# One GpSimd product per unit instead of two, softplus spread over three units, and gates behind the fourth scan, in a selective-scan kernel on one core

## What is computed

```python
x = x + 0.5 * ffn(layernorm(x))       # int4-quantized weight, bias, low-rank part
x = x + ssm(layernorm(x))             # below; 512 channels, 64 states each
x = x + 0.5 * ffn(layernorm(x))

# ssm, for each sequence
h = layernorm(x) * norm_w + norm_b
u, z = split(h @ Win)                 # 512 and 512 channels
u = silu(causal_conv4(u) + conv_b)
dt = softplus(u @ dt_w + dt_b)
B, C = u @ Bp, u @ Cp                 # 64 states each
state[d, s] = state[d, s] * exp(dt[d] * A[d, s]) + dt[d] * u[d] * B[s]    # over time
y[d] = sum_s state[d, s] * C[s]
out = x + ((y + u * D) * silu(z)) @ Wout
```

## Time and profile before

| | us |
|---|---|
| median of 3 runs | 5270.37 (5265.89 to 6636.7) |
| the profiled execution, its time | 5275.21 |
| its span, first to last instruction | 5272.6 |

### The profile page before, as it was taken

How to read it: one execution, slowest core, us unless ns; L and a number is a source line. 1 busy time by engine, 2 the same in 40 slices (tenths; PEclk the granted TensorE clock), 3 DMA queues, 4 the chain that set the end, 5 groups by cost and what they waited for, 6 DMA issues and landing times.

```text
span 5272.6 us, 189257 instructions
## 1 busy us (share of the span) xinstructions
PE 4814.2 (91%) x85070; PEld 2906.2 (55%) x85070; DVE 4915.5 (93%) x4674; ACT 3854.6 (73%) x6536; POOL 5021.0 (95%) x2312
## 2 busy tenths in 40 slices
PE   7989989899898999989999898998989989999887
PEld 4555555555555555555555555555555555555554
DVE  7999999999999999999999999999999999999996
ACT  5687777778777787777767778777787777766564
POOL 4999999999999999999999999999999999999997
PEclk8999999999999999999999999999999999999999
DMA  8755666556565565655656566565655656557543
GB/s 217 194 187 192 170 204 177 193 178 185 187 177 191 180 185 191 173 201 183 176 193 169 201 177 186 189 179 190 180 191 187 175 194 176 187 180 183 191 178 117
DMA packets 578058, 970.78 MB, mean 184 GB/s; under 512 B 294593, under 2 KB 328162, under 8 KB 511714
## 3 DMA queue, kind: packets, MB, share of 16 engines
q1 hardware_dynamic: 327394, 948.32, 56.4%
q10 hardware_dynamic: 249856, 10.36, 3.6%
HBM read 872.60 MB, written 85.98 MB: 182 GB/s over the span
## 4 chain that ended last, share of the span: by engine, by line
PE 35%; POOL 28%; DVE 20%; issue 10%; ACT 4%; DMA 3%; SPq 1%; DVEq 0%; POOLq 0%; ACTq 0%
POOL H L866 24%; DVE H L645 17%; PE pUB L972 14%; PE Y L998 12%; PE pP L936 3%; PE pP L930 3%; DVE cv L596 2%; ACT dA L422 2%; DMA Bd<-scratch_diag 2%; POOL dto L847 1%; POOL duo L853 1%; POOL lnv L842 1%; PE pA L1012 1%; DMA scratch_ut<-uto 1%; ACT L422 1%
## 5 line engine op out<-in xcount | busy, mean ns | idle before, releaser
L866 POOL TENSOR_TENSOR H<-H,Cb 128x1024 f32<-128x1024 f32 x2048 | 4782.6, 2379 | 151.1 <-DVE H L645 134.0
L645 DVE TENSOR_TENSOR_SCAN H<-dA,pUB 128x512 f32<-128x512 f32 x4096 | 4639.7, 1198 | 238.8 <-PE pUB L972 213.8
L422 ACT ACTIVATE dA<-DT,w_negA 128x512 f32<-128x512 f32 x4096 | 2620.1, 711 | 1230.9 <-DVE H L645 1227.2
L972 PEld LDWEIGHTS pUB<-Bd,UT 64*64 64x64 f32 x65536 | 1873.1, 134 | 1428.4 <-DVE H L645 682.7
L972 PE MATMUL pUB<-Bd,UT 64*64 64x128 f32 x65536 | 2243.4, 275 | 404.7 <-DVE H L645 321.5
L998 PE MATMUL Y<-H,w_ident 64*64 64x512 f32 x16384 | 1970.3, 595 | 9.9 <-POOL H L866 5.0
L998 PEld LDWEIGHTS Y<-H,w_ident 64*64 64x64 f32 x16384 | 599.5, 135 | 614.7 <-issue 601.7
L930 PE MATMUL pP<-hT,w_Win 128*128 128x512 f32 x480 | 239.3, 621 | 0.0
L936 PE MATMUL pP<-U,w_dt_w 128*128 128x512 f32 x480 | 238.1, 618 | 0.0
L422 ACT ACT_TABLE_LOAD x178 | 228.4, 1283 | 11.3 <-DVE H L645 4.7
L1012 PE MATMUL pA<-w_Wf,XNT 128*128 128x256 f32 x496 | 142.7, 412 | 7.5 <-DVE X L600 6.1
(11 more groups left out here) (151 smaller groups left out, 1750.3 us busy)
## 6 DMA issues: line engine op xcount, KB each, us to landing
Cb<-scratch_c SPq DMA_DIRECT2D x512, 1024.0 KB, 5.2
Bd<-scratch_diag SPq DMA_DIRECT2D x510, 512.0 KB, 6.2
ZL<-scratch_z SPq DMA_DIRECT2D x64, 256.0 KB, 6.7
scratch_z<-zo SPq DMA_DIRECT2D x62, 256.0 KB, 5.7
scratch_dt<-dto SPq DMA_DIRECT2D x60, 256.0 KB, 6.8
scratch_ut<-uto SPq DMA_DIRECT2D x60, 256.0 KB, 5.6
DT<-scratch_dt SPq DMA_DIRECT2D x60, 256.0 KB, 5.0
UT<-scratch_ut SPq DMA_DIRECT2D x60, 256.0 KB, 5.6
```

The lines of the kernel that those rows point to most:

```text
L422: last = nc.scalar.activation(dA[:, n % DAR, j, :], DT[:, k, :], ACT.Exp, scale=c["negA"][:, k, GS * blk + j:GS * blk + j + 1])
L645: last = nc.vector.tensor_tensor_scan(H[:, u % HR, 2 * i + j, :], dA[:, n % DAR, 2 * i + j, :], pUB[:, i, :].rearrange("p (t s) -> p s t", ...
L866: nc.gpsimd.tensor_tensor(h[:, j:j + 2, :], h[:, j:j + 2, :], Cb[:, blk % 2, j:j + 2, :], ALU.mult).then_inc(times_c, 1)
L972: last = nc.tensor.matmul(out, UT[rows, k, j * P + h * HP:j * P + h * HP + HP], Bd[rows, blk % 2, i, j * P:(j + 1) * P].rearrange("p (t s) ...
```

## The change

GpSimd waits for all four scans of a unit and multiplies the four states in one operation of 128x2048; `times_c` still rises by two per unit. The three softplus operations stand behind the products of three units (table POOLS: "less" at 32, 38, 46, 54, "dt" one unit later, "du" two later). The gates move from behind the second scan to behind the fourth, in the same units.

```diff
@@ -36,7 +36,7 @@
         "norm 3": (49, 50, 51, 55), "turn 1": (25, 27), "turn c": (38, 41), "turn 3": (58, 62)}
 DVES = {"norm 1": (6,), "norm c": (26,), "norm 2": (43,), "norm 3": (51,), "soft": (31, 37, 45, 53),
         "conv": (2, 7, 12, 17), "x2": (13, 20), "x1": (30, 34), "out": (44, 46)}
-POOLS = {"dt": (32, 38, 46, 54), "du": (33, 39, 47, 55)}
+POOLS = {"less": (32, 38, 46, 54), "dt": (33, 39, 47, 55), "du": (34, 40, 48, 56)}
 PES = {"xs": (0, 5, 10, 15), "z": (3, 8, 13, 18), "BC": ((20, 22),), "turn b": (24,), "dt": ((26, 28), (32, 34), (40, 42), (48, 50)),
        "turn u": (38, 46, 54, 59), "turn 1": (23, 25), "turn c": (36, 39), "turn 3": (56, 60)}
 LATER = {"y": ((7, 12), (17, 19)), "ffn 1": ((27, 29), (31, 33)), "ffn c": ((41, 43), (44, 45))}
@@ -603,10 +603,10 @@
 
                 c_, q, a = b - 1, b + 1, b + 2
                 when = DVES
-                if close and n == 3 and i == 1:
+                if close and n == 3 and i == 3:
                     gate(c_, 2)
                     gate(c_, 3)
-                if scan and n == HALF + 3 and i == 1:
+                if scan and n == HALF + 3 and i == 3:
                     gate(b, 0)
                     gate(b, 1)
                 if proj and n in when["conv"] and i:
@@ -860,14 +860,13 @@
                     if scan:
                         if n % 2 == 0:
                             pool.wait_ge(c_in[blk % 2], at(16 * (b * NBLK + n // 4 + 1)))
-                    for j in range(0, GS, 2):
-                        if scan:
-                            pool.wait_ge(state_done, at(2 * (GN * b + n) + j // 2 + 1))
-                            nc.gpsimd.tensor_tensor(h[:, j:j + 2, :], h[:, j:j + 2, :], Cb[:, blk % 2, j:j + 2, :], ALU.mult).then_inc(times_c, 1)
-                        if proj and n in when["dt"]:
-                            sum_dt(q, when["dt"].index(n), j // 2)
-                        if proj and n in when["du"] and j == 0:
-                            times_u(q, when["du"].index(n))
+                        pool.wait_ge(state_done, at(2 * (GN * b + n) + 2))
+                        nc.gpsimd.tensor_tensor(h, h, Cb[:, blk % 2], ALU.mult).then_inc(times_c, 2)
+                    for part, what in enumerate(("less", "dt")):
+                        if proj and n in when[what]:
+                            sum_dt(q, when[what].index(n), part)
+                    if proj and n in when["du"]:
+                        times_u(q, when["du"].index(n))
                     if close and n in turns["norm c"]:
                         shift_of(nc, pool, flipc, normc[0], normc[3], normc[4], c_)
                     if ffn and n in turns["norm 1"]:
```

## The result

The changed kernel takes 5186.56 us (median of four runs, 5184.62 to 5194.16) against 5270.61 us before: a ratio of 0.9846, with a 95% interval of 0.9829 to 0.9863. The ratio is that of the mean times, without one execution before that took 6636.7 us; the medians give 0.9841. That is 84 us less, where the sum said 78, and 5187 where 5192 was forecast. The profiled execution took 5194.16 us, its span 5192.2 against 5272.6.

A forecast was written before the change was run, and what follows sets the result against it. Each step was bound by VectorE and TensorE for units 0 to 37, then GpSimd for 38 to 61. 15 x (3.8 + 1.2) plus 3 gave 78 us less: 5192 us, range 5152 to 5262.

The forecast's parts named there:

- Price of the product: GpSimd's product with C: one 128x2048 operation takes 4.51 us against 4.648 for two, saving 0.14 us per unit.
- The rival in which nothing of the start is saved: GpSimd's product stays at 4.65 us per unit; the kernel takes 5260 us; chance 0.12.
- the one in which the long product is dearer: Units 32 to 61: product costs more than two short ones, kernel slower from 4.68 us, up to 5408; chance 0.07.
- Later entry: GpSimd waits for all four states of unit 32, so its stretch starts 2.1 us later each step.
- Phase two: GpSimd's stretch with softplus work, counted from unit 32 to 61: no waits, 1.3 us margin at unit 38, 3.8 us gained per step.
- Gate of unit 3: VectorE's wait for TensorE's last sum goes, 1.0 us a step, plus 0.2 for what follows.
- Softplus spread, SP's wait, the dt of ACT: Softplus over three units, SP's 1.2 us at unit 56's dt store, ACT's dt ready 0.8 us early: all cost nothing.
- The sums of odd units: TensorE's sums in odd units wait 2.3 us more for a whole product; covered, 1 us per step if not.
- The last step: Step without softplus, GpSimd's throughout: 9 us could go, VectorE's end caps it, less 2 us: 3 us gained.
- The signs: Expected in the trace: starts 4.51 us apart, more GpSimd idle before gapless units 32 to 61, gates' idle 15, chain entry near 32.
- Given back at the handover: Rival: transfers and SP's new wait hold units 60, 62, 66; half of 3.8 us lost, 5220 us; chance 0.16.
- more than summed: Rival: TensorE's clock around unit 3 recovers, up to 1.6 us; with products at 4.45, 8.4 a step, 5140 us; chance 0.12.

## Why the prediction was right, and where it wasn't

- **Price of the product: right.** 4.51 us from start to start was taken from a slope between two sizes; nine distances of 4.50 were measured. The rival in which nothing of the start is saved (4.65) and the one in which the long product is dearer (4.68 and more) fall with it. Merging two operations into one brought 67 us, where 72 follows from 0.14 a unit.
- **Later entry: right.** 2.1 us a step; the wait for all four states cost 28 us by itself, where 31 was counted.
- **Phase two: the length right, its division wrong.** 150.4 us from unit 32's start to unit 61's end was worked out, 150.3 came in step 5 and 150.8 in the mean of 15 steps; the second part of a step lost 3.8 us, as summed. The failing step is this: "The 1.88 at unit 35 lies in front of GpSimd's phase and gives nothing by itself; it is what buys the margin above." I let phase two begin at unit 38 in the kernel before, because the chain entered there, compared its length from unit 32 on with a phase without gaps, and booked the whole 4.0 us to the product. But 1.93 of them are the gaps at units 37 and 38 that come from the gates' place. So of 4.0 a step some 2.1 are the product's (30 x 0.14 - 2.1) and 1.9 the gates'; over 15 steps the runs with one edit each give 2.0 and 1.8. With the numbers of step 5 the product alone should then bring 15 x 2.1 + 3 = 35 us, and 35 was measured (the exact match is luck, as the last step brings 5.0 of it and not 3); the gates 15 x (1.9 + 1.2) = 47, and 41 was measured. The sum was right because the stretch was counted once and correctly; whoever takes its terms as prices of single edits is 25 us off for the product and 23 for the gates. The waits that it did see at unit 35 were also read too small: it took 1.88, and the 2.02 behind it in the earlier trace rows belongs to the same place.
- **Gate of unit 3: mis-sized as a single edit.** It had 1.0 + 0.2 a step. With the other gate in place it is worth 6 us, 0.4 a step. The first part of a step did lose 1.0 us with both gates moved. But "What follows now, a wait of 0.33 us at unit 5, goes too" failed: in step 5 of the changed kernel that wait is there, and longer, in VectorE's timeline:

```profile
1701.83 4.55 DVE L645 TENSOR_TENSOR_SCAN H<-dA,pUB 128x512 f32<-128x512 f32 x4 [1.21 <-PE pUB L971]
```

Of 1.76 + 0.33 before, 0.9 are gone, where 2.1 were to go. As a mean over the steps the sum had 1.2 for both waits, and 1.0 came.
- **Gates' waits: better than said.** One is left (12.3 us), as the 15 us forecast amounts to.
- **Softplus spread, SP's wait, the dt of ACT: nothing, as costed.** Spread in or out makes 0 and 4 us in two pairs. SP waits 0.79 us at each of the four stores of a step, where one wait of 1.2 was counted, and moving the last store away from Bd brings nothing. ACT's dt wasn't tested alone; it is inside the spread's nothing.
- **The sums of odd units: right here, and no more than just.** TensorE's waits for products are small in the changed kernel, and 46 us once Bd is earlier.
- **The last step: mis-sized, and the cap is what failed.** 3 us were given. From the first scan of step 15 to the end it takes 336.2 us instead of 343.7: 7.5 less. Two of its three terms came out: counted from that scan, the products end 9.3 us earlier (9 were counted), and the stretch behind them is 1.9 us longer (2 were counted). What failed is "VectorE caps it". GpSimd's lag behind VectorE did fall by only 3.4, from 9.4 to 6.0 (rows below), but VectorE's own end came 5.9 us earlier. That is the gates': its units 2 to 5 take 19.0 us instead of 21.8 and its units 32 to 39 36.8 instead of 39.7, and with one gate back that gate's stretch is 20.2 or 39.7 again.
- **The signs.** Starts 4.50 apart: seen. GpSimd's idle time grew: 151.1 to 210.2. No gap from unit 33 to 61: seen in step 5 and in 11 more of 15; the other three have 0.2, 1.6 and 1.7 us of gaps. Gates: seen. The chain's entry near unit 32: not seen; it enters at unit 45. That is no sign of a second limit. GpSimd has no gap from unit 32 on, and VectorE's scans of units 33 to 45 end 1.2 to 4.9 us before GpSimd starts their product. The chain's releasers are inferred from semaphore events, and at 1906.97, where GpSimd starts unit 45's product right behind unit 44's, the chain steps to scans of unit 46 that end at 1906.91, for which this product doesn't wait. The gaps are the better sign than the chain's entry.
- **Given back at the handover: not seen.** The second part of a step, which has the handover in it, lost the 3.8 us in full, so the transfers at its end kept nothing back.
- **The total.** 15 x (1.0 + 3.8) = 72 us by the table, where 75 were summed, and 7.5 for the last step, where 3 were: these two misses go against each other, and that the forecast came within 6 us is in part luck.
- **Granted clock.** The rival "more than summed" rested on the 0.60 around unit 3. It had said against itself that the idle time there isn't touched, and that is what came. Two stretches of 4 us there show 0.74 and 0.83 in the changed kernel. They split the low stretch between them: the clock missing is (0.26 + 0.17) x 4 = 1.7 us, and before, with 0.60 and then 0.97 in the next 4 us, it was (0.40 + 0.03) x 4 = 1.7 as well. TensorE's wait for VectorE ahead of it is 2.43 us in both. Over the steps the clock did rise at units 34 to 38 (1.3 us missing a step before, none now) and 56 to 63 (1.2 and 0.1), both in the second part of a step, which gained what the sum had for it and no more. The gain was 6 us over the sum, far from that rival's 5140. Busy time by stretch, changed kernel (behind POOL's stand the clock, DMA share, GB/s):

```profile
1688.00:1692.00 4.00, 2.06 (x36) 2.01 (x40) 4.00 (x6) 2.08 (x4) 4.00 (x2) 0.74 0.09 34
1692.00:1696.00 4.00, 4.00 (x50) 1.82 (x43) 4.00 (x5) 3.43 (x11) 4.00 (x1) 0.83 0.77 276
```

The end of step 15 in the changed kernel, first VectorE's timeline, then GpSimd's:

```profile
5108.89 37.86 DVE L645 TENSOR_TENSOR_SCAN H<-dA,pUB 128x512 f32<-128x512 f32 x34
...
5089.65 63.08 POOL L864 TENSOR_TENSOR H<-H,Cb 128x2048 f32<-128x2048 f32 x14
```

The scans end at 5146.75, the products at 5152.73: the lag of 6.0 us.

## What to carry to other kernels

When a phase is counted as one engine's, compare its full length before and after from the same unit on, and then look in the old timeline for gaps inside it: each gap belongs to the edit that closes it, not to the engine's new price. Price two edits that touch one stretch singly too, since a right sum can hide two wrong terms, and the terms decide which edit is kept. Merging operations on a queue buys the fixed part of each start and pays with a later first and a coarser release; here 67 us against 28. And where a wait is priced, look for the next one behind it: here an engine that had to pause also lost clock, and the wait after the pause was as long as the one before it.

## What the hardware showed beyond what was expected

- A VectorE tensor_tensor with two SBUF inputs beside a full GpSimd queue can lose to the running product and to the one or two queued behind it: 0.67 us alone, up to 6.79 us beside products of 4.5 us and 5.53 beside those of 2.3. Where it comes first it costs 0.67 us, and the product beside it 4.81 instead of 4.55.
- GpSimd's elementwise operation on two fp32 tiles takes 1.23, 2.32 and 4.50 us from start to start for 512, 1024 and 2048 columns, a straight line with some 0.14 us at no columns.
- TensorE's granted clock fell behind a pause of 2.77 us at unit 35 (0.64 in the 4 us that followed, 1.00 before), and stayed at 1.00 in the kernel in which the pause is gone.
- Bd's load of 512 KB lands 6.7 us after its issue (median) on SP's queue behind the load of C, and 4.3 us on ACT's.
